# Attention in two halves: key scores two a step in steps 0 to 7, the next unit's query scores two a step in steps 7 to 14

## The chip, the cores and the metric

The kernel runs on one core of a Trainium2 chip. The time is that of the whole program on the device, in microseconds (us); the figure for a kernel is the median of several runs. The profiled execution is a run of its own with its own time. The engines are PE (TensorE, matmuls), DVE (VectorE), ACT (ScalarE), POOL (GpSimd) and SP (SyncE, which issues all DMAs here). Each works through its own instructions in order and waits on semaphores for the others.

## What is computed

One decoder layer on a batch of 8 sequences of 512 rows and 512 columns: self-attention with 16 heads of 32 columns, a retention layer, a coupling network; after each a residual sum and a layer norm. The change is in the attention alone:

```python
kv = (_ln(x, kvn_w, kvn_b) @ kv_w + kv_b).reshape(b, c, 2, HEAD, HD).transpose(2, 0, 3, 1, 4)
k, v = kv[0], kv[1]
q = (_ln(x, qn_w, qn_b) @ q_w + q_b).reshape(b, c, HEAD, HD).transpose(0, 2, 1, 3)
q, k = _rotary(q, x, rh_w, rh_b), _rotary(k, x, rh_w, rh_b)
qn, kn = _ln(q, ln_w, ln_b), _ln(k, ln_w, ln_b)
scores = jnp.einsum('bhqd,bhkd->bhqk', qn, kn) / np.sqrt(HD)
attn = jax.nn.softmax(scores, axis=-1)
a = jnp.einsum('bhqk,bhkd->bhqd', attn, v).transpose(0, 2, 1, 3).reshape(b, c, dims)
return a @ out_w + out_b
```

## The kernel before

The attention phase is 32 units U = 4b + g: batch b of 8, and g one of four groups of four heads. A unit has 16 steps, and tables at the top of the file (lines 31 to 42) say at which step each piece of work stands; every engine runs its own `unit` function over the same steps, so the tables set the order of instructions on each engine. All semaphore waits follow from that order.

Three units are in work at once. In unit U:

- For U itself PE does 16 *key scores* (line 741, bank `exp`), ACT an exponential for each (line 632), and after every four of them PE *weighs* (line 752): eight matmuls for the output and eight for the sums, both of a quarter of the array's width. DVE *normalises* in four chunks (lines 475 and 477), ACT and DVE split the result into a high and a low part (lines 639 and 486). `weigh` of the next unit's first quarter waits for that low part (line 748).
- For U + 1 PE does 16 *query scores* (line 726, banks `max0` and `max1`), DVE takes a row maximum of each (line 467). Query score i waits for maximum i - 2 (two banks). When all 16 are done PE transposes the maxima (line 732), ACT copies them into `stack` (`save_max`, line 623), and only then can the key scores of U + 1 begin (line 738).
- For U + 3 PE projects: 16 items of three matmuls (lines 703 to 705), four items for each of four row tiles t; DVE adds the bias (`save_qkv`, lines 431 and 433); tile t waits for the save of tile t - 2. POOL rotates.
- For U + 2 DVE takes means and variances of the heads (lines 439 and 449), POOL subtracts and scales (lines 305 to 320), PE turns the heads (line 714), ACT and DVE split them (`turn_high`, line 619; `turn_low`, line 458). After the second `turn_low` SP issues 24 DMAs that lay the parts of unit U + 2 out in `stack` (`regroup`, line 227). Query scores of a head wait for its six DMAs.

In the unit with g = 0 of batch b PE also multiplies the attention of batch b - 1 with the output weights (`project_out`, lines 760 to 762, four tiles of 12 matmuls), and transposes the normalised rows of batch b + 1 (line 696). In the unit with g = 1 SP, behind its 24 DMAs, loads residual rows (line 238) and then the rows `z` of batch b + 2 (line 241). In the unit with g = 2 DVE takes the statistics of these rows (`x_stats`, lines 382 and 383), whose first instruction waits for that load (line 381); this is done for b = 0 to 5. In the unit with g = 3 follow `x_final` and `x_shift`.

The loop over steps on DVE has this order within one step:

```python
row_max of U + 1; normalise (if its step is below 8); attn_low (line 486); head_mean; head_var;
save_qkv; turn_low; x_stats; x_final; x_shift; add_out; z_low; normalise (if its step is 8 or more)
```

and on PE: query scores, projection items, key scores, `weigh`, transposed maxima, turned heads, transposed rows, output products.

Of the kernel before, what the change touches and what calls it, by code (L numbers as in the profile page):

```python
# [19 lines left out]
B, S, D = 8, 512, 512  # L20
T = S // P
K = D // P
H, HD = 16, 32
G = 4
HG = H // G
# [2 lines left out]
DVE_STEPS, POOL_STEPS = 55, 40  # L28


QS_DONE = tuple(T * HG * min(i + 1, 14) // 14 for i in range(16))
KS_DONE = tuple(T * HG * min(i, 12) // 12 for i in range(16))
PROJECT_DONE = (3, 5, 6, 8, 10, 11, 13, 15, 16, 16, 16, 16, 16, 16, 16, 16)
WEIGH_AT = (5, 8, 11, 14)
TURN_AT, SAVE_AFTER = (9, 11), (2, 4, 7, 9)
OUT_AT, ADD_AFTER, OUT_BANK = (10, 12, 15, 15), (11, 13, 15, 15), (1, 1, 0, 1)
Z_AT, Z_HIGH_AT, Z_LOW_AFTER = (13, 13, 14, 14), (13, 13, 15, 15), (13, 14, 15, 15)
MAX_AT, SAVE_MAX_AT = 14, 14
X_NORM_AT, STATS_AFTER, FINAL_AFTER, SHIFT_AFTER = (5, 6, 7, 8), (6, 8, 10, 12), 6, 12
MEAN_AFTER, VAR_AFTER, SQUARE_AT = (0, 1), (3, 4), (1, 2)  # L40
TURN_HIGH_AT, TURN_LOW_AFTER = (10, 12), (11, 13)
NORM_AFTER, ATTN_HIGH_AT, ATTN_LOW_AFTER = (15, 15, 0, 1), 2, 3
SIDES = (1, 0)

ROW = 3 * HD
# [46 lines left out]
def attention_phase(nc, x, x1, w):  # L92
# [6 lines left out]
    with ctx:  # L99
# [264 lines left out]
        def _(dve):  # L364
# [105 lines left out]
            def normalise(W, c):  # L470

                at = slice(c * P, (c + 1) * P)
                if c == 0:
                    dve.wait_ge(pv_done, T * W + T)
                nc.vector.reciprocal(inverse[:, at], bank_sum[:, at]).then_inc(dve_step, 1)  # L475
                dve.wait_ge(dve_step, steps.next())
                last = nc.vector.tensor_tensor(bank_o[:, at], bank_o[:, at], inverse[:, at], ALU.mult)
                if c < T - 1:
                    last.then_inc(dve_step, 1)
                    dve.wait_ge(dve_step, steps.next())  # L480
                else:
                    last.then_inc(attn_done, 1)
# [12 lines left out]
            def unit(b, g, left, more):  # L495
                U = G * b + g
                for i in range(T * HG):
                    if left >= 1:
                        for m in within(QS_DONE, i):
                            row_max(U + 1, m)  # L500
# [83 lines left out]
            for s in range(2):  # L584
                turn_low(1, s, bank_t[s])
            run(dve, unit, steps, DVE_STEPS)
            for c in range(2, T):
                normalise(G * B - 1, c)
            attn_low(G * B - 1, G - 1)
            for t in range(T):  # L590
                add_out(B - 1, t)
# [2 lines left out]
        def _(act):  # L594
# [46 lines left out]
            def unit(b, g, left, more):  # L641
                U = G * b + g
                for i in range(T * HG):
                    for m in within(KS_DONE, i):
                        exps(U, m)
                    if i == ATTN_HIGH_AT and counts(U):
                        attn_hi(U - 1, (g - 1) % G)
                    for s in range(2):
                        if left >= 2 and i == SQUARE_AT[s]:
                            square(U + 2, s)  # L650
                        if left >= 2 and i == TURN_HIGH_AT[s]:
                            turn_high(U + 2, s, bank_t[0 if g == 0 else s])
                    for t in range(T):
                        if g == 0 and left == 4 and i == X_NORM_AT[t]:
                            x_norm(b + 1, t)
                        if g == 0 and left == 4 and i == Z_HIGH_AT[t]:
                            z_high(b + 1, t)
                    if i == SAVE_MAX_AT and left >= 1:
                        save_max(U + 1, (g + 1) % 2)

            act.wait_ge(load, 16 * len(loads))
            for t in range(T):
# [26 lines left out]
        def _(pe):  # L689
# [131 lines left out]
            def unit(b, g, left, more):  # L821
                U = G * b + g
                for i in range(T * HG):
# [6 lines left out]
                    for m in within(KS_DONE, i):  # L830
                        key_scores(U, g % 2, m)
                    if i in WEIGH_AT:
                        weigh(U, g, WEIGH_AT.index(i))
# [1105 lines left out]
```

## Time and profile before

| what | value |
|---|---|
| median of 3 runs | 2420.73 us (2419.41 to 2424.11) |
| profiled execution, its own time | 2423.02 us |
| its span | 2421.0 us |
| mean granted TensorE clock | 0.901 |
| PE busy | 1945.1 us (80%) |
| DVE busy | 1546.8 us (64%) |
| ACT busy | 908.2 us (38%) |
| POOL busy | 951.5 us (39%) |

The attention phase fills about the first 1300 us of the span. A row of a timeline gives the start, the duration, the engine, the line, the operation with the names of the tiles, how many instructions were merged (x), and in brackets for how long the engine had been idle and what released it. Matmuls overlap: the start of one to the start of the next is what it really takes, not the duration shown. PEclk is the granted clock as a share of 2.4 GHz; 0.5 is 1.2 GHz.

### The profile page before, as it was taken

How to read it: one execution, taken by the hardware profiler on the slowest of the kernel's cores; microseconds unless marked ns; L12 is line 12 of the kernel's file. 1: busy time of each engine (PE TensorE's matmuls, PEld its weight loads, DVE VectorE, ACT ScalarE, POOL GpSimd, SP SyncE). 2: the span in 40 equal slices, each digit the busy share in tenths (PEclk: the TensorE clock that was granted, in tenths of full speed). 3: DMA queues.
4: the chain of work that ended last, by engine and by line, in shares of the span. 5: the costliest groups of instructions: out<-in, count | busy, mean ns of one | idle time of the engine just before them, and what ended most of it. 6: DMA issues, size and time to landing. Idle time of an engine off the chain costs nothing. (4 is left out here: it accounts for less than half of the span.)

```text
span 2421.0 us, 30214 instructions
## 1 busy us (share of the span) xinstructions
PE 1945.1 (80%) x9560; PEld 1426.2 (59%) x9560; DVE 1546.8 (64%) x2943; ACT 908.2 (38%) x1532; POOL 951.5 (39%) x849
## 2 busy tenths in 40 slices
PE   4587887878888798788975799999948887788772
PEld 4455565555656465565633688888837665666651
DVE  4567667576675666767562666667654776767765
ACT  2143433334333343334341322222214555555653
POOL 1666756467564674746620222222201212221221
PEclk9688998989989898999987899999979999989985
DMA  3123132131311212222122211211031121022111
GB/s 128 26 53 87 37 94 48 48 85 36 95 47 50 77 36 74 69 57 70 38 77 101 78 53 60 79 69 53 18 107 37 52 70 49 22 69 70 53 35 52
DMA packets 90746, 148.67 MB, mean 61 GB/s; under 512 B 16560, under 2 KB 19632, under 8 KB 90672
## 3 DMA queue, kind: packets, MB, share of 16 engines
q1 hardware_dynamic: 90672, 147.76, 20.5%
q8 instruction: 37, 0.61, 0.1%
q14 instruction: 37, 0.30, 0.0%
HBM read 63.82 MB, written 33.55 MB: 40 GB/s over the span
## 5 line engine op out<-in xcount | busy, mean ns | idle before, releaser
L467 DVE TENSOR_REDUCE a_neg_max<-a_max 128x1 f32<-128x512 f32 x512 | 344.5, 687 | 267.3 <-PE a_max L726 258.8
L632 ACT ACTIVATE a_probs<-a_exp 128x512 f32<-128x512 f32 x512 | 290.7, 595 | 571.1 <-PE a_exp L741 568.5
L726 PE MATMUL a_max<-a_stack 96*128 96x512 f32 x512 | 235.9, 476 | 150.7 <-DMA a_stack<-a_nT_lo 100.6
L726 PEld LDWEIGHTS a_max<-a_stack 96*128 96x128 f32 x512 | 103.2, 206 | 245.4 <-DMA a_stack<-a_nT_lo 106.8
L1497 POOL TENSOR_TENSOR f_mixed<-f_tw,f_beta 128x512 f32<-128x512 f32 x64 | 96.1, 1522 | 352.2 <-DVE f_beta L1596 177.0
L311 POOL TENSOR_TENSOR a_rstd<-a_rstd,a_minus_half 128x16 f32<-128x16 f32 x64 | 186.5, 2914 | 85.0 <-DVE a_rstd L452 85.0
L703 PE MATMUL a_t<-a_w_hi,a_zT_hi 128*128 128x384 f32 x512 | 196.5, 384 | 13.4 <-DVE a_v L433 11.5
L741 PE MATMUL a_exp<-a_stack 100*128 100x512 f32 x512 | 193.5, 419 | 6.5 <-ACT a_probs L632 4.5
L704 PE MATMUL a_t<-a_w_lo,a_zT_hi 128*128 128x384 f32 x512 | 194.8, 380 | 0.0
L705 PE MATMUL a_t<-a_w_hi,a_zT_lo 128*128 128x384 f32 x512 | 193.0, 377 | 0.0
L305 POOL TENSOR_TENSOR a_n<-a_n,a_mean 128x512 f32<-128x512 f32 x64 | 67.2, 1050 | 309.8 <-DVE a_mean L441 309.6
L1767 PE MATMUL f_l<-f_h_hi,f_w_hi 128*128 128x512 f32 x240 | 111.3, 464 | 73.1 <-DVE f_h_lo L1510 72.4
L1047 POOL TENSOR_TENSOR r_part<-r_part 128x512 f32<-128x512 f32 x32 | 45.8, 1432 | 315.1 <-DVE r_part L1094 315.1
L752 PE MATMUL a_o<-a_probs,a_v 128*32 128x512 f32 x1024 | 140.7, 622 | 3.3 <-ACT a_probs L632 0.9
L475 DVE RECIPROCAL a_inverse<-a_sum 128x128 f32<-128x128 f32 x128 | 121.8, 951 | 30.4 <-PE a_sum L752 29.2
L752 PE MATMUL a_sum<-a_probs,a_ones 128*32 128x512 f32 x1024 | 137.2, 608 | 0.0
L703 PEld LDWEIGHTS a_t<-a_w_hi,a_zT_hi 128*128 128x128 f32 x512 | 114.1, 223 | 23.8 <-DVE a_v L433 13.0
L1510 DVE TENSOR_TENSOR f_h_lo<-f_full,f_h_hi 128x512 fp32r<-128x512 f32 x104 | 70.4, 689 | 81.2 <-ACT f_h_hi L1675 80.5
L704 PEld LDWEIGHTS a_t<-a_w_lo,a_zT_hi 128*128 128x128 f32 x512 | 114.0, 223 | 13.5
L1169 ACT ACTIVATE r_kq_hi<-r_part 128x512 fp32r<-128x512 f32 x64 | 36.8, 624 | 218.7 <-POOL r_part L1048 218.7
L741 PEld LDWEIGHTS a_exp<-a_stack 100*128 100x128 f32 x512 | 101.9, 201 | 26.3 <-ACT a_probs L632 13.6
L705 PEld LDWEIGHTS a_t<-a_w_hi,a_zT_lo 128*128 128x128 f32 x512 | 113.5, 222 | 0.0
(240 smaller groups left out, 4865.7 us busy)
## 6 DMA issues: line engine op xcount, KB each, us to landing
a_stack<-a_nT_hi SPq DMA_DIRECT2D x512, 64.0 KB, 2.0
a_stack<-a_nT_lo SPq DMA_DIRECT2D x256, 64.0 KB, 2.0
a_z<-x SPq DMA_DIRECT2D x8, 1024.0 KB, 7.4
a_y<-x SPq DMA_DIRECT2D x8, 1024.0 KB, 5.5
x<-a_y SPq DMA_DIRECT2D x8, 1024.0 KB, 4.4
r_xn<-x SPq DMA_DIRECT2D x8, 1024.0 KB, 5.6
r_cn<-ctx SPq DMA_DIRECT2D x8, 1024.0 KB, 7.7
x<-r_xn SPq DMA_DIRECT2D x8, 1024.0 KB, 4.3
```

The lines of the kernel that those rows point to most:

```text
L311: nc.gpsimd.tensor_tensor(rstd[:, c], rstd[:, c], minus_half[:, :], ALU.pow).then_inc(pool_step, 1)
L467: nc.vector.tensor_reduce(neg_max[:, t, ROW + h:ROW + h + 1], bank_max[i % 2][:, :], AX_X, ALU.max, negate=True).then_inc(max_done, 1)
L475: nc.vector.reciprocal(inverse[:, at], bank_sum[:, at]).then_inc(dve_step, 1)
L632: nc.scalar.activation(probs[:, kt % 2, h, :], bank_exp[i % 2][:, :], ACT.Exp, scale=float(1.0 / np.sqrt(np.float32(HD)))).then_inc(exp_do ...
L703: mm(bank, zT_hi[:, k, at], w_hi[:, k, g, :], start=k == 0, stop=False)
L704: mm(bank, zT_hi[:, k, at], w_lo[:, k, g, :], start=False, stop=False)
L705: last = mm(bank, zT_lo[:, k, at], w_hi[:, k, g, :], start=False, stop=k == K - 1)
L726: mm(bank_max[i % 2][:, :], stack[0:ROW, par, h, t * P:(t + 1) * P], stack[0:ROW, par, HG + h, :], start=True, stop=True).then_inc(score_d ...
L741: mm(bank_exp[i % 2][:, :], stack[0:ROW + HG, par, HG + h, kt * P:(kt + 1) * P], stack[0:ROW + HG, par, h, :], start=True, stop=True).then ...
L752: last = mm(bank[at, :], ones[:, :] if sums else v[:, g, kt, at], probs[:, kt % 2, h, :], start=kt == 0, stop=kt == T - 1, tile_position=( ...
L1497: nc.gpsimd.tensor_tensor(mixed[:, j % 2, :], tw[:, par, j, :], beta[:, :], ALU.mult).then_inc(product_done, 1)
L1767: mm(bank, a_hi, b_hi, start=first, stop=False)
```

## The change

The tables give every piece another step. Key scores stood about three in four steps in steps 1 to 12 and query scores about eight in seven in steps 0 to 13, so that the two alternated. Now all 16 key scores stand two a step in steps 0 to 7 and all 16 query scores two a step in steps 7 to 14. `weigh` moves from steps 5, 8, 11, 14 to 3, 5, 7, 9; the maxima are transposed in step 15; the first three chunks of `normalise` come in steps 12, 13 and 15 of the unit itself and the last in step 0 of the next; `x_stats` moves from steps 6, 8, 10, 12 to 0, 1, 2, 3 of the unit with g = 2; `x_norm`, `x_final`, the turned heads and the output products move by some steps. No instruction is added or left out.

```diff
-QS_DONE = tuple(T * HG * min(i + 1, 14) // 14 for i in range(16))
-KS_DONE = tuple(T * HG * min(i, 12) // 12 for i in range(16))
-PROJECT_DONE = (3, 5, 6, 8, 10, 11, 13, 15, 16, 16, 16, 16, 16, 16, 16, 16)
-WEIGH_AT = (5, 8, 11, 14)
-TURN_AT, SAVE_AFTER = (9, 11), (2, 4, 7, 9)
-OUT_AT, ADD_AFTER, OUT_BANK = (10, 12, 15, 15), (11, 13, 15, 15), (1, 1, 0, 1)
+KS_DONE = tuple(2 * min(i + 1, 8) for i in range(16))
+QS_DONE = tuple(2 * max(min(i - 6, 8), 0) for i in range(16))
+PROJECT_DONE = (3, 6, 8, 8, 10, 10, 12, 12, 14, 15, 16, 16, 16, 16, 16, 16)
+WEIGH_AT = (3, 5, 7, 9)
+TURN_AT, SAVE_AFTER = (11, 12), (2, 4, 7, 11)
+OUT_AT, ADD_AFTER, OUT_BANK = (11, 12, 15, 15), (12, 13, 15, 15), (1, 1, 0, 1)
...
-MAX_AT, SAVE_MAX_AT = 14, 14
-X_NORM_AT, STATS_AFTER, FINAL_AFTER, SHIFT_AFTER = (5, 6, 7, 8), (6, 8, 10, 12), 6, 12
+MAX_AT, SAVE_MAX_AT = 15, 15
+X_NORM_AT, STATS_AFTER, FINAL_AFTER, SHIFT_AFTER = (10, 10, 11, 11), (0, 1, 2, 3), 3, 12
...
-TURN_HIGH_AT, TURN_LOW_AFTER = (10, 12), (11, 13)
-NORM_AFTER, ATTN_HIGH_AT, ATTN_LOW_AFTER = (15, 15, 0, 1), 2, 3
+TURN_HIGH_AT, TURN_LOW_AFTER = (11, 12), (11, 13)
+NORM_AFTER, ATTN_HIGH_AT, ATTN_LOW_AFTER = (12, 13, 15, 0), 1, 1
...
-            for c in range(2, T):
-                normalise(G * B - 1, c)
+            normalise(G * B - 1, T - 1)
...
+                    if i == SAVE_MAX_AT and left >= 1:
+                        save_max(U + 1, (g + 1) % 2)
                     for t in range(T):
                         if g == 0 and left == 4 and i == X_NORM_AT[t]:
                             x_norm(b + 1, t)
                         if g == 0 and left == 4 and i == Z_HIGH_AT[t]:
                             z_high(b + 1, t)
-                    if i == SAVE_MAX_AT and left >= 1:
-                        save_max(U + 1, (g + 1) % 2)
```

DVE at the place where the first `x_stats` stands in the unit with g = 2, before (L467 is a row maximum, L382 and L383 the statistics of `z`):

```order
L467 TENSOR_REDUCE a_neg_max<-a_max 128x1
L463 REGISTER_ALU
L467 TENSOR_REDUCE a_neg_max<-a_max 128x1
L463 REGISTER_ALU
L467 TENSOR_REDUCE a_neg_max<-a_max 128x1
L381 ISA
L382 BN_STATS a_stats<-a_z 128x6
L383 SCALAR_TENSOR_TENSOR a_inverse,a_per_step<-a_z,a_rh_w 128x512
L386 REGISTER_ALU
L463 REGISTER_ALU
L467 TENSOR_REDUCE a_neg_max<-a_max 128x1
```

The same place now (L475 and L477 are the last chunk of `normalise`, L439 and L441 the first `head_mean`, L486 is `attn_low`):

```order
L475 RECIPROCAL a_inverse<-a_sum 128x128
L476 REGISTER_ALU
L477 TENSOR_TENSOR a_o<-a_o,a_inverse 128x128
L438 REGISTER_ALU
L439 TENSOR_REDUCE a_mean<-a_n 128x16
L440 REGISTER_ALU
L441 TENSOR_SCALAR a_mean<-a_mean 128x16
L381 ISA
L382 BN_STATS a_stats<-a_z 128x6
L383 SCALAR_TENSOR_TENSOR a_inverse,a_per_step<-a_z,a_rh_w 128x512
L386 REGISTER_ALU
L486 TENSOR_TENSOR a_attnT_lo<-a_o,a_attnT_hi 128x512
```

The statistics stood behind the seventh or eighth row maximum of the unit; they now stand ahead of all of them, and ahead of `attn_low`.

PE near the end of a unit with g = 1, before (L726 is a query score, L741 a key score, L752 `weigh`, L714 turned heads, L732 the transposed maxima):

```order
L714 MATMUL a_t<-a_ident,a_n 128x128 x4
L725 REGISTER_ALU
L726 MATMUL a_max<-a_stack 128x512
L741 MATMUL a_exp<-a_stack 128x512 x2
L725 REGISTER_ALU
L726 MATMUL a_max<-a_stack 128x512
L725 REGISTER_ALU
L726 MATMUL a_max<-a_stack 128x512
L746 REGISTER_ALU
L752 MATMUL a_o<-a_probs,a_v 32x512 x4
L752 MATMUL a_sum<-a_probs,a_ones 32x512 x4
L732 MATMUL a_max<-a_ident,a_neg_max 100x128 x4
```

PE in the middle of a unit now (lines of this engine's part are lower by one: L725 is a query score, L740 a key score, L751 `weigh`, L702 to L704 a projection item):

```order
L740 MATMUL a_exp<-a_stack 128x512 x2
L720 REGISTER_ALU
L725 MATMUL a_max<-a_stack 128x512 x2
L740 MATMUL a_exp<-a_stack 128x512 x2
L751 MATMUL a_o<-a_probs,a_v 32x512 x4
L751 MATMUL a_sum<-a_probs,a_ones 32x512 x4
L724 REGISTER_ALU
L725 MATMUL a_max<-a_stack 128x512
L724 REGISTER_ALU
L725 MATMUL a_max<-a_stack 128x512
L770 REGISTER_ALU
L702 MATMUL a_t<-a_w_hi,a_zT_hi 128x384
```

The two kinds of scores no longer alternate; the first two query scores come just ahead of the last two key scores and the third `weigh`, and all others behind.

## Rows read from the trace of the kernel before

**Rows 1.** Windows of five units: length, PE, PEld, DVE, ACT, POOL busy, PEclk, DMA.

```profile
572.32:615.60 43.28, 39.02 (x222) 27.79 (x221) 23.43 (x44) 18.23 (x30) 20.22 (x19) 1.00 0.22 51
615.60:653.40 37.80, 30.65 (x157) 20.77 (x157) 26.66 (x52) 13.39 (x22) 22.23 (x21) 0.86 0.18 53
653.40:692.01 38.61, 30.69 (x157) 19.27 (x157) 26.99 (x57) 13.33 (x22) 24.99 (x22) 0.82 0.33 95
692.01:724.67 32.66, 28.60 (x157) 19.52 (x157) 24.34 (x56) 13.29 (x22) 24.57 (x23) 0.90 0.22 52
1111.46:1142.92 31.46, 27.33 (x157) 18.34 (x157) 22.27 (x45) 13.29 (x22) 23.37 (x22) 0.95 0.33 84
```

**Rows 2.** Groups by line: busy, mean ns | idle before, releasers.

```profile
L467 DVE TENSOR_REDUCE a_neg_max<-a_max 128x1 f32<-128x512 f32 x512 | 344.5, 687 | 267.3 <-PE a_max L726 258.8 <-DVE a_o L477 3.8 <-DVE a_inverse L383 1.1
L726 PE MATMUL a_max<-a_stack 96*128 96x512 f32 x512 | 235.9, 476 | 150.7 <-DMA a_stack<-a_nT_lo 100.6 <-DVE a_neg_max L467 48.5
```

**Rows 3.** PE's timeline across the end of a unit with g = 2.

```profile
681.43 0.64 PE L732 MATMUL a_max<-a_ident,a_neg_max 128*100 128x128 f32 x4
687.13 0.80 PE L726 MATMUL a_max<-a_stack 96*128 96x512 f32 x1 [5.05 <-DMA a_stack<-a_nT_lo]
692.01 0.39 PE L741 MATMUL a_exp<-a_stack 100*128 100x512 f32 x1
```

**Rows 4.** DVE's timeline: second turn_low of g = 1, first x_stats of g = 2.

```profile
642.76 0.68 DVE L458 TENSOR_TENSOR a_nT_lo<-a_t,a_nT_hi 128x512 fp32r<-128x512 f32 x1
...
666.99 0.69 DVE L382 BATCH_NORM_STATS2 a_stats<-a_z 128x6 f32<-128x512 f32 x1 [4.33 <-DMA a_z<-x]
...
668.40 0.69 DVE L467 TENSOR_REDUCE a_neg_max<-a_max 128x1 f32<-128x512 f32 x1
```

**Rows 5.** SP's timeline: first and last issue of regroup in g = 1, load of z.

```profile
643.47 0.53 SPq L227 DMA_DIRECT2D a_stack<-a_nT_hi  x1
...
657.98 0.59 SPq L227 DMA_DIRECT2D a_stack<-a_nT_lo  x1
...
659.52 0.38 SPq L241 DMA_DIRECT2D a_z<-x  x1
```

**Rows 6.** PE's timeline: weigh and items at full clock, weigh at half.

```profile
658.98 1.06 PE L752 MATMUL a_o<-a_probs,a_v 128*32 128x512 f32 x8
...
660.84 0.73 PE L726 MATMUL a_max<-a_stack 96*128 96x512 f32 x2
661.41 0.35 PE L703 MATMUL a_t<-a_w_hi,a_zT_hi 128*128 128x384 f32 x1
661.94 0.34 PE L703 MATMUL a_t<-a_w_hi,a_zT_hi 128*128 128x384 f32 x1
...
673.44 1.94 PE L752 MATMUL a_o<-a_probs,a_v 128*32 128x512 f32 x8
```

**Rows 7.** ACT's timeline: save_max, one exponential, three back to back.

```profile
682.11 1.87 ACT L623 ACTIVATE a_stack<-a_max 4x2048 fp32r<-4x2048 f32 x1 [2.29 <-PE a_max L732]
692.44 0.60 ACT L632 ACTIVATE a_probs<-a_exp 128x512 f32<-128x512 f32 x1 [8.46 <-PE a_exp L741]
695.54 1.78 ACT L632 ACTIVATE a_probs<-a_exp 128x512 f32<-128x512 f32 x3
```

**Rows 8.** Groups by line in the unit from 692.01 to 724.67.

```profile
L475 DVE RECIPROCAL a_inverse<-a_sum 128x128 f32<-128x128 f32 x5 | 4.8, 951 | 0.8 <-PE a_sum L752 0.8
L431 DVE TENSOR_TENSOR a_qk<-a_t,a_qkv_bias 128x256 f32<-128x256 f32 x4 | 1.7, 417 | 0.0
L477 DVE TENSOR_TENSOR a_o<-a_o,a_inverse 128x128 f32<-128x128 f32 x5 | 1.5, 300 | 0.2
```

**Rows 9.** PE's timeline at the end of a unit with g = 0.

```profile
602.89 0.64 PE L732 MATMUL a_max<-a_ident,a_neg_max 128*100 128x128 f32 x4
...
606.84 0.50 PE L760 MATMUL a_t<-a_wo_hi,a_attnT_hi 128*128 128x512 f32 x1 [2.43 <-DVE a_zT_lo L422]
...
612.28 0.39 PE L762 MATMUL a_t<-a_wo_hi,a_attnT_lo 128*128 128x512 f32 x1
```

## The prediction

> **What bounds the kernel now.** I read first the windows by unit [rows 1], since every engine's order repeats unit by unit. A batch of four units takes 152.3 us. No engine fills its unit: in the one from 692.01 PE shows 28.6 of 32.7 us, DVE 24.3, POOL 24.6, ACT 13.3. So the order and its waits set the pace, not one engine. The units differ: g = 0 carries output products and transposes (43.3), g = 1 and 2 take 37.8 and 38.6, g = 3 32.7, and a unit of batch 6, where no `z` is loaded, 31.5. Then the groups by line [rows 2]: PE's largest wait in attention is for the DMAs that fill `stack`, 100.6 us ahead of query scores, and DVE waits 258.8 us for query scores. The timelines [rows 3, 4, 5] show where: a unit begins with a query score that waits 5.05 us for its DMAs, and the first `x_stats` waits 4.33 us for `z`.
>
> **What the change takes away.** Query scores now begin at step 7. SP starts `regroup` right after the second `turn_low` and is through with 24 issues in 15.1 us (643.47 to 658.57) [rows 5]; below the first query score comes some 19 us after that `turn_low`, and each head's DMAs are ahead of it. I cost the `stack` wait at nothing from here on: up to 100.6 us gone, over 31 units 3.2 each.
>
> **The regular unit, step by step.** Time 0 is the end of its predecessor's sixteenth row maximum. Prices at full clock: a score 0.23; an item of three matmuls 0.53 (661.41 to 661.94) and a `weigh` 1.86 (658.98 to 660.84) [rows 6]; an exponential 0.59 when they queue (1.78 for three), its result usable about 1.0 after its score's start (692.01, 692.44, 0.60) [rows 3, 7]; a row maximum 0.61 to 0.69 [rows 2]; a chunk of `normalise` 1.3 (0.95 and 0.30 with a wait between) and a `save_qkv` about 0.6 [rows 8]; a `turn_low` 0.68 [rows 4].
>
> First the boundary: transposed maxima, then `save_max` 0.68 after their start and 1.87 long [rows 3, 7]. That puts the first key score at 2.75; three items hide most of it. Steps 0 to 3: eight key scores wait for exponentials two before them, while ACT also does `attn_hi` and two squares, the second of which waits for POOL behind `attn_low` and the second mean on DVE. Key 7 goes at 8.4, `weigh` 0 at 8.6 to 10.5. Two items, keys 8 and 9 (12.0), key 10 behind exponential 8 (12.6), key 11, `weigh` 1 to 15.3, two items, keys 12 and 13 to 16.8. Query score 0 goes at 16.9. Keys 14 and 15 wait for exponentials 12 and 13; `weigh` 2 ends at 20.0. DVE has had its two maxima and a save by 18.9 and idles to 20.4: query 2 stands behind `weigh` 2. The same again at `weigh` 3 (22.5 to 24.4): maximum 6 starts at 24.8. From there DVE is the chain: ten maxima (6.5), the last save (0.6), two `turn_low` (1.3), two chunks of `normalise` in steps 12 and 13 (2.6), less what two banks allow PE to run ahead, and a short wait at the turned heads: the sixteenth maximum ends at 35.4. So a regular unit takes 35.5 us, against 32.7 and 31.5 for g = 3 and for batch 6, and 37.8 for g = 1. What is late in place of `stack` is DVE: its 10 us of maxima no longer run beside the key scores, and it has little to do in steps 0 to 6. POOL's 24.6 us [rows 1] fit inside 35.5; I cost its reordering at nothing. If its rotation (behind the fourth save, now step 11, before 9) sets the means of the next unit, up to 2 us a unit more; since the first half there waits for ACT anyway, I take 0.
>
> **g = 0.** In the second half the two output tiles cost PE 2.8 each (24 matmuls in 5.7 us, 606.84 to 612.5 [rows 9]), and each stands ahead of query scores that DVE waits for; with additions and `z_low` on DVE the sixteenth maximum ends near 43.0. The transposed maxima wait for a bank until 44.3; from there to the end of the last two output tiles it took 9.6 us (602.89 to 612.5) [rows 9], an order that is unchanged; three items, and the next key score at 55.3: a length of 52.5, against 43.3.
>
> **g = 2: the rows of z.** This is the largest term. `x_stats` now stands in step 0, ahead of `attn_low`, and `weigh` 0 waits for `attn_low`. `z` cannot come earlier: it is issued behind the 24 DMAs of `regroup`, 16.1 us after the end of `turn_low` in g = 1 (643.44 to 659.52), and DVE goes on with it at 666.99, 23.6 after that end [rows 4, 5]. In the new order that `turn_low` ends 2.5 us before time 0, so `z` is there at 21.0. `x_stats` takes 1.4 (666.99 to 668.40), `attn_low` 0.7: `weigh` 0 goes at 23.1 and not at 8.6, 14.5 later, and behind it are PE's items, all query scores and so everything. PE stands still for it; after the shorter wait of 5.05 us in [rows 3] its matmuls ran 0.80 long, and at half clock (1.2 GHz) half a `weigh` is 1.94 long where it is 1.06 at full clock (2.4 GHz) [rows 6]; I add 2. The unit takes 52, against 38.6. The remaining three `x_stats` and the delayed means lie on DVE in the first half, where it has room.
>
> [...]
>
> **The sum.** A full batch: 52.5 + 35.5 + 52 + 35.5 = 175.5 against 152.3, +23.2. Batches 1 to 5: +116. Batch 6 has no `z`: +9.2 - 2.3 + 4 + 4 = +15. Batch 0 has no output products, and its first key score no longer stands behind the first fill of `stack`: about +12. Batch 7 has no items and shrinks to few differences: +3. Together +146 at the prices of full clock. The granted clock in units that are less dense is lower: 0.82 with 30.7 busy of 38.6, 0.95 with 27.3 of 31.5 [rows 1]. The new unit has the same matmuls in 35.5. Bounds: nothing more, or, with a second half wholly at half clock, +4 (two `weigh` at +1.7, the rest partly hidden by DVE). I take +1, near the rows of today, +31 over 31 units. The phases behind attention are untouched. So +177 on the profiled execution's own 2423.0 (span 2421.0): 2600; the median is 2.3 lower, hence 2598.
>
> **The rivals.**
> 1. *Only the late z costs.* Regular units and g = 0 stay as long as now, because the freed `stack` waits pay for DVE's new idleness in full. For it: 3.2 us a unit are gone, and my regular unit differs from today's by only -2 to +4. Against: the two waits behind `weigh` and the serial boundary follow from the order. Then 6 times 13.4 (52 against 38.6), +80: 2500.
> 2. *The clock falls.* DVE paces the second half, PE runs in short bursts and is granted 1.2 GHz through most of it: +4 a unit in place of +1, some +93 more: 2690. [...] The rows agree in direction (0.82 to 0.95 above), but a clock of 1.00 with 39.0 busy of 43.3 and 0.90 with 28.6 of 32.7 leave most units at the full level.
> 3. *Faster.* The query scores no longer wait for `stack`, and the halves overlap better than I have it: DVE's work of one unit's end runs beside the next one's key scores, and a regular unit comes down to what PE has at full clock (32 scores 7.4, 16 items 8.4, four `weigh` 7.4, turns and maxima 1.3) plus the boundary and two waits, 28. A batch is then 28 x 4 + 16 + 17 = 145, -7; over the phase about -40: 2380. It decides from a regular unit below 29.8, (152.3 - 33) / 4. For it: PE has 24.5 us of work. Against: it would need DVE to do the 15 us between query 0 and maximum 15 without a wait, and ACT to be no bound in steps 0 to 3. The late `z` remains even so.
>
> **How the numbers follow.** A difference of 0.2%, about 5 us, is what a measurement can tell from none. Forecast 0.52, with its own range 2545 to 2655; only the late z 0.25; the clock 0.13; faster 0.08; the remaining 0.02 is a coincidence of gains and losses within 0.2%. Slower is 0.90, same 0.02, faster 0.08. The range leaves out the faster case and the far part of the clock case: 2480 to 2695.
>
> **What would show it.** In the profile after: one wait of DVE's line 382 for `z` of 15 to 18 us in each of six batches, where it is 4.33 now; PE's wait of the same place some 14 us, ahead of `weigh`, with half clock behind it. No wait of query scores for `stack` beyond a few us. Row maxima that wait for query scores twice in a unit, at the third and fourth `weigh`. Units from key score to key score near 52, 35, 52, 35. I am wrong if `z` lands within a few us of DVE's arrival, if regular units are under 32, or if they are over 38 at a clock above 0.85.

## The result: 12% slower, and 116 us slower than forecast

| | before | changed |
|---|---|---|
| median, run side by side | 2422.42 us (2419.41 to 2427.52, 4 runs) | 2713.65 us (2711.63 to 2715.52, 4 runs) |
| ratio, 95% interval | 1 | 1.120 (1.1177 to 1.1222) |
| profiled execution, its span | 2423.02, 2421.0 | 2715.52, 2713.5 |
| mean granted TensorE clock | 0.901 | 0.867 |

The direction was as forecast. The size was not: +291 us where the text had +177, and the time lies above the range's upper end of 2695.

The busy times and the instruction queue, from the profile page of the changed kernel:

```profile
PE 2071.6 (76%) x9560; PEld 1437.7 (53%) x9560; DVE 1554.1 (57%) x2943; ACT 905.9 (33%) x1532; POOL 944.6 (35%) x849
...
q14 instruction: 62, 0.51, 0.1%
```

PE shows 126 us more of busy time for the same 9560 matmuls. At half clock they run longer: eight matmuls of a `weigh` 1.94 us in place of 1.06 (below). The row of q14, one of the two queues of the kind `instruction`, was not read ahead of the prediction. It counts 62 packets; the page of before has 37.

Windows of the four units of batch 3, of a unit of batch 6, and of the phase from the first key score of all to the last unit's (columns as in [rows 1]):

```profile
690.08:746.66 56.58, 45.69 (x222) 30.34 (x221) 25.00 (x46) 18.25 (x30) 20.98 (x20) 0.88 0.20 46
746.66:792.04 45.38, 32.98 (x157) 19.04 (x157) 24.80 (x49) 13.28 (x22) 21.57 (x21) 0.86 0.12 36
792.04:845.57 53.53, 34.31 (x158) 20.09 (x157) 28.46 (x56) 13.17 (x22) 23.14 (x22) 0.76 0.25 69
845.57:884.55 38.98, 31.87 (x158) 19.33 (x157) 24.26 (x55) 13.16 (x22) 24.89 (x25) 0.89 0.17 41
...
1368.23:1406.47 38.24, 31.69 (x157) 19.12 (x157) 23.25 (x44) 13.16 (x22) 22.81 (x22) 0.90 0.27 69
...
121.98:1564.15 1442.17, 1089.38 (x5172) 655.64 (x5171) 769.23 (x1507) 442.02 (x733) 675.89 (x632) 0.85 0.19 49
```

The same stretch of the kernel before:

```profile
131.07:1269.18 1138.11, 961.81 (x5165) 642.43 (x5164) 756.16 (x1497) 444.22 (x733) 677.35 (x625) 0.91 0.24 62
```

The phase is 304 us longer and starts 9 us earlier; what lies behind it is 2.5 us shorter. All four kinds of units grew, and the fourth kind, the last row but one, is what a unit costs in which nothing is special: 38.2 us, against 31.5 in [rows 1]. From the mean clock c of a stretch of length L one gets the time at the lower of the two levels (PEclk 0.50) as 2(1 - c)L: about 2 x 0.09 x 1138 = 205 us before and 2 x 0.15 x 1442 = 433 us now. That there are two levels is what short windows show: of 3793 windows of 0.3 us in this stretch of the kernel before, 3095 have a PEclk of 1.00 and 627 one of 0.50; of 4806 in that of the changed kernel, 3277 and 1441; the rest lie between the two.

The groups by line, which answer to [rows 2]:

```profile
L467 DVE TENSOR_REDUCE a_neg_max<-a_max 128x1 f32<-128x512 f32 x512 | 329.4, 685 | 346.4 <-PE a_max L725 340.4
...
L725 PE MATMUL a_max<-a_stack 96*128 96x512 f32 x512 | 222.4, 485 | 69.3 <-DVE a_neg_max L467 59.7
...
L751 PE MATMUL a_o<-a_probs,a_v 128*32 128x512 f32 x1024 | 148.5, 654 | 79.1 <-DVE a_attnT_lo L486 79.1
```

The 100.6 us that query scores waited for `stack` are gone, as forecast. In their place DVE waits 340.4 us for query scores (258.8 before), and PE 79.1 us for `attn_low`, in six waits.

**The late `z`.** DVE's timeline: the second `turn_low` of g = 1, the first `x_stats` of g = 2, and `attn_low` behind it:

```profile
784.93 0.68 DVE L458 TENSOR_TENSOR a_nT_lo<-a_t,a_nT_hi 128x512 fp32r<-128x512 f32 x1
...
809.15 0.69 DVE L382 BATCH_NORM_STATS2 a_stats<-a_z 128x6 f32<-128x512 f32 x1 [17.62 <-DMA a_z<-x]
...
810.48 0.69 DVE L486 TENSOR_TENSOR a_attnT_lo<-a_o,a_attnT_hi 128x512 fp32r<-128x512 f32 x1
```

SP's timeline between them, and PE's at the same place:

```profile
785.64 0.54 SPq L227 DMA_DIRECT2D a_stack<-a_nT_hi  x1
...
801.69 0.38 SPq L241 DMA_DIRECT2D a_z<-x  x1
```

```profile
811.31 1.94 PE L751 MATMUL a_o<-a_probs,a_v 128*32 128x512 f32 x8 [12.90 <-DVE a_attnT_lo L486]
```

From the end of `turn_low` to the first `x_stats` are 23.6 us, the number of [rows 4, 5]. PE stands for 12.90 us where 14.5 were booked, and `weigh` behind it runs at half clock: half of it is 1.94 long where it is 1.06 at full clock [rows 6].

**The regular unit.** PE's timeline in batch 6, g = 2; the prediction's time 0 is 1364.32 here, where the sixteenth maximum ends:

```profile
1364.46 1.09 PE L731 MATMUL a_max<-a_ident,a_neg_max 128*100 128x128 f32 x4 [2.32 <-DVE a_neg_max L467]
...
1366.31 0.52 PE L702 MATMUL a_t<-a_w_hi,a_zT_hi 128*128 128x384 f32 x1
...
1367.27 0.52 PE L702 MATMUL a_t<-a_w_hi,a_zT_hi 128*128 128x384 f32 x1
...
1368.23 1.05 PE L740 MATMUL a_exp<-a_stack 100*128 100x512 f32 x2
...
1374.84 1.06 PE L751 MATMUL a_o<-a_probs,a_v 128*32 128x512 f32 x8
...
1383.39 0.63 PE L725 MATMUL a_max<-a_stack 96*128 96x512 f32 x2
```

and DVE's, later in the unit:

```profile
1387.37 1.29 DVE L467 TENSOR_REDUCE a_neg_max<-a_max 128x1 f32<-128x512 f32 x2 [1.73 <-PE a_max L725]
...
1392.05 2.63 DVE L467 TENSOR_REDUCE a_neg_max<-a_max 128x1 f32<-128x512 f32 x4 [1.88 <-PE a_max L725]
...
1402.57 0.95 DVE L475 RECIPROCAL a_inverse<-a_sum 128x128 f32<-128x128 f32 x1
```

The items at the boundary follow each other in 0.96 us, at half clock, where 0.53 was booked [rows 6]. The first key score comes at 3.9 (booked 2.75), `weigh` 0 at 10.5 (8.6), query 0 at 19.1 (16.9), maximum 6 at 27.7 (24.8), and the sixteenth ends at 38.25 (35.4). The two waits behind `weigh` 2 and 3 are there, 1.73 and 1.88. Two thirds of the loss of 2.85 us have arisen by `weigh` 0: 1.2 up to the first key score, and 0.8 more between that and `weigh` 0.

The lower level does not begin with the wait of 2.32 us ahead of the transposed maxima, which lasts from 1362.14 to 1364.46. It begins earlier, among the last query scores, where PE waits for row maxima. PE's windows and timeline there:

```profile
1349.01:1359.25 10.24, 9.29 (x48) 5.08 (x46) 7.95 (x14) 1.19 (x2) 2.12 (x3) 1.00 0.00 0
1359.25:1369.49 10.24, 6.49 (x20) 5.39 (x20) 8.20 (x15) 2.41 (x3) 7.54 (x11) 0.50 0.29 66
```

```profile
1358.32 1.01 PE L725 MATMUL a_max<-a_stack 96*128 96x512 f32 x2 [0.63 <-DVE a_neg_max L467]
1360.75 1.39 PE L725 MATMUL a_max<-a_stack 96*128 96x512 f32 x2 [1.42 <-DVE a_neg_max L467]
```

Two scores took 1.01 us there, and the next two 1.39.

**A hole that nobody releases.** DVE's timeline at the start of the unit with g = 1:

```profile
746.95 0.30 DVE L477 TENSOR_TENSOR a_o<-a_o,a_inverse 128x128 f32<-128x128 f32 x1
753.03 0.96 DVE L475 RECIPROCAL a_inverse<-a_sum 128x128 f32<-128x128 f32 x1 [5.78 <-issue]
```

Between two chunks of `normalise` DVE stands still for 5.78 us and waits for nothing that the profile shows (the releaser is "issue"). PE's key scores behind it then wait 6.58 us for an exponential. The loop over batches runs six times, and each pass begins with the unit with g = 1; the hole stands behind each of the five jumps back (5.78 to 5.83 us), and nowhere else in DVE's program of this phase. 62 - 37 = 25 more packets of instructions are five a jump. The trace also records the branches: at each of these jumps DVE's next instruction starts 5.40 to 5.44 us behind the branch, and 0.26 to 0.30 behind it in the kernel before. The unit takes 45.4 us in batches 1 to 5, and 37.9 in batch 6, behind the loop.

### The profile page after: what moved, and what is told of

Read it like the earlier page. It is cut to its first block and busy times, and to the rows that moved or that the text cites. A ratio compares the mean times of both kernels' runs of the same rounds, so it can differ in the third digit from the quotient of the medians.

```text
span 2713.5 us, 30240 instructions
## 1 busy us (share of the span) xinstructions
PE 2071.6 (76%) x9560; PEld 1437.7 (53%) x9560; DVE 1554.1 (57%) x2943; ACT 905.9 (33%) x1532; POOL 944.6 (35%) x849
## 5 line engine op out<-in xcount | busy, mean ns | idle before, releaser
L467 DVE TENSOR_REDUCE a_neg_max<-a_max 128x1 f32<-128x512 f32 x512 | 329.4, 685 | 346.4 <-PE a_max L725 340.4
L631 ACT ACTIVATE a_probs<-a_exp 128x512 f32<-128x512 f32 x512 | 277.9, 596 | 296.1 <-PE a_exp L740 289.4
L725 PE MATMUL a_max<-a_stack 96*128 96x512 f32 x512 | 222.4, 485 | 69.3 <-DVE a_neg_max L467 59.7
L740 PE MATMUL a_exp<-a_stack 100*128 100x512 f32 x512 | 209.7, 467 | 80.9 <-ACT a_probs L631 76.6
L702 PE MATMUL a_t<-a_w_hi,a_zT_hi 128*128 128x384 f32 x512 | 202.0, 395 | 16.2 <-DVE a_v L433 11.7
L751 PE MATMUL a_o<-a_probs,a_v 128*32 128x512 f32 x1024 | 148.5, 654 | 79.1 <-DVE a_attnT_lo L486 79.1
L725 PEld LDWEIGHTS a_max<-a_stack 96*128 96x128 f32 x512 | 95.3, 197 | 194.8 <-DVE a_neg_max L467 125.6
L740 PEld LDWEIGHTS a_exp<-a_stack 100*128 100x128 f32 x512 | 103.1, 206 | 163.0 <-ACT a_probs L631 150.4
L704 PE MATMUL a_t<-a_w_hi,a_zT_lo 128*128 128x384 f32 x512 | 188.4, 368 | 0.0
L702 PEld LDWEIGHTS a_t<-a_w_hi,a_zT_hi 128*128 128x128 f32 x512 | 111.3, 217 | 81.6 <-issue 52.2
L475 DVE RECIPROCAL a_inverse<-a_sum 128x128 f32<-128x128 f32 x128 | 121.5, 949 | 45.3 <-issue 29.0
L751 PE MATMUL a_sum<-a_probs,a_ones 128*32 128x512 f32 x1024 | 145.3, 641 | 0.0
L622 ACT ACTIVATE a_stack<-a_max 4x2048 fp32r<-4x2048 f32 x32 | 59.8, 1870 | 251.3 <-PE a_max L731 251.3
L287 POOL TENSOR_TENSOR a_turn<-a_qk,a_cos 128x256 f32<-128x256 f32 x64 | 47.5, 742 | 273.9 <-DVE a_v L433 273.9
L618 ACT ACTIVATE a_nT_hi<-a_t 128x512 fp32r<-128x512 f32 x64 | 38.2, 597 | 313.1 <-PE a_t L713 313.0
```

Of the source, the lines that this page charges most:

```text
L467: nc.vector.tensor_reduce(neg_max[:, t, ROW + h:ROW + h + 1], bank_max[i % 2][:, :], AX_X, ALU.max, negate=True).then_inc(max_done, 1)
L631: nc.scalar.activation(probs[:, kt % 2, h, :], bank_exp[i % 2][:, :], ACT.Exp, scale=float(1.0 / np.sqrt(np.float32(HD)))).then_inc(exp_do ...
L702: mm(bank, zT_hi[:, k, at], w_hi[:, k, g, :], start=k == 0, stop=False)
L704: last = mm(bank, zT_lo[:, k, at], w_hi[:, k, g, :], start=False, stop=k == K - 1)
L725: mm(bank_max[i % 2][:, :], stack[0:ROW, par, h, t * P:(t + 1) * P], stack[0:ROW, par, HG + h, :], start=True, stop=True).then_inc(score_d ...
L740: mm(bank_exp[i % 2][:, :], stack[0:ROW + HG, par, HG + h, kt * P:(kt + 1) * P], stack[0:ROW + HG, par, h, :], start=True, stop=True).then ...
```

## The experiments

After the result there were four places to which 291 us could belong: the late `z`; the hole behind the jump back; DVE's and PE's other work in the second half; and what remains when all these are taken away, the order of two halves and the clock that it leaves. Numbers 1, 4, 5, 10 and 11 ask for the first (theory A: it costs its full time wherever it stands), 2, 3 and 9 for the second (theory C: it belongs to the loop's place among the instructions, not to its work), 6, 7 and 12 for the third (theory F: DVE's chunks), 8 and 11 for the last. The times of before beside each are those of runs on the same chip, 2422 to 2428 us. In the expectations `after_late` is number 1, `halves_norm` number 6 and `early_q2` number 8.

**1. The statistics one unit later.** `z` is then there long before it is wanted.

```diff
-                    if g == 2 and more and i in STATS_AFTER:
+                    if g == 3 and more and i in STATS_AFTER:
```

> The changed kernel with x_stats in steps 0 to 3 of the unit with g = 3 instead of g = 2, so that DVE never stands for the load of z ahead of attn_low. Theory A (the late z is the largest single cost of the change): the wait of line 382 goes, a unit with g = 2 falls from 53.5 to the 38.2 us that it takes in batch 6 where no z is loaded, six times 15.3, so 2714 - 92 = 2622 us; four statistics (5.6 us of DVE) fit in the first half of g = 3, where DVE waits anyway. Theory B (DVE's work is what is short, not z): g = 3 grows by the 5.6 us, six times, and the gain is 58 us: 2656.

Measured: 2611.61 us, ratio 1.0773 (1.0749 to 1.0797), 102 less than the changed kernel. The unit with g = 2 shrinks from 53.5 to 38.4 us. The late `z` costs about 15 us six times, and no other wait takes its place.

**2. DVE's loop four places earlier.** The unit written out ahead of the loop now has three chunks of `normalise` instead of two (steps 12, 13 and 15 against 15 and 15), so that the loop begins later in DVE's program. DVE does the same 2943 instructions of work in both kernels, but with waits and register instructions counted, the trace has 576 of DVE's records ahead of the first branch back where it had 569, and 377 in a pass of the loop where it had 374. So the loop begins four instructions later, and not two, and its end stands seven later. Four copies instead of eight ahead of the loop do the same work with four instructions less:

```diff
-            for half in range(2):
-                for h in range(HG):
-                    last = nc.vector.tensor_copy(stack[ROW:ROW + HG, half, HG + h, :],
-                                                 ident[ROW:ROW + HG, ROW + h:ROW + h + 1].broadcast_to((HG, S)))
+            for h in range(HG):
+                last = nc.vector.tensor_copy(stack[ROW:ROW + HG, :, HG + h, :],
+                                             ident[ROW:ROW + HG, ROW + h:ROW + h + 1].unsqueeze(1).broadcast_to((HG, 2, S)))
```

> The changed kernel with four instead of eight copies on DVE ahead of the attention loop (two stack halves in one copy), so that the loop begins four instructions earlier; nothing in the loop is touched. [...] Theory D (the hole is a wait that the profile doesn't name): unchanged, 2714.

Measured: 2677.26 us, ratio 1.1046 (1.1022 to 1.1071), 36 less; five units that fall from 45.4 to the 37.9 of batch 6 would give 37.5. From its page, and the window of batch 4, g = 1:

```profile
q14 instruction: 37, 0.30, 0.0%
```

```profile
1107.77:1145.97 38.20, 31.55 (x157) 18.89 (x157) 24.88 (x49) 13.28 (x22) 21.54 (x21) 0.88 0.13 42
```

The 25 packets and the hole are gone, the unit falls from 45.4 to 38.2. The loop's work is unchanged, so the hole belongs to where the loop lies.

**3. The kernel before with two more instructions ahead of the loop.**

```diff
+            for i in range(2):
+                nc.vector.memset(pad[:, i:i + 1], 0.0)
```

> The kernel before with two one-column memsets on DVE ahead of the attention loop; nothing in the loop is touched. Theory C: 25 instruction packets more, a hole of about 6 us on DVE at each of five jumps back. There the next row maximum is what PE waits for, so up to 6 us each: 2422 + 30 = 2452 us. Theory D: unchanged, 2422.

Measured: 2425.81 us, ratio 1.0009 (0.9995 to 1.0023), 38 packets. No stop behind the jump back (0.24 to 0.30 us, the table under number 9) and no cost: two places alone don't do it in this kernel. The two were too few to reproduce the change, which moves the branch back by seven; number 9 goes further.

**4. The kernel before with the statistics in steps 0 to 3.**

```diff
-X_NORM_AT, STATS_AFTER, FINAL_AFTER, SHIFT_AFTER = (5, 6, 7, 8), (6, 8, 10, 12), 6, 12
+X_NORM_AT, STATS_AFTER, FINAL_AFTER, SHIFT_AFTER = (5, 6, 7, 8), (0, 1, 2, 3), 6, 12
```

> The kernel before with STATS_AFTER at steps 0 to 3 instead of 6, 8, 10, 12, and nothing else of the change. Theory A: z lands some 24 us after turn_low in this order too, DVE stands from about 6 us after it, PE stands at the third query score and at weigh 0; a unit with g = 2 grows by 13 to 18 us, six times: 2500 to 2530 us. Theory E (the alternating order absorbs the wait, since key scores and items run on): under 2450.

Measured: 2509.22 us, ratio 1.0355 (1.0328 to 1.0382), +85, near 14 us a load. Its table of waits:

```profile
DVE a_stats L382 <- DMA a_z<-x: 90.1, 6, 15.4
```

The units with g = 2 take 52 to 54 us where they took 37.5 to 40.5. So the early statistics cost nearly the same alone, in the old order.

**5. The load of `z` ahead of the 24 DMAs of `regroup`.**

```diff
+                if g == 1 and more:
+                    sp.wait_ge(zT_done, T * (b + 2))
+                    sp.dma_start(z[:, :, :], rows(x, b + 2)).then_inc(x_in, 16)
...
-                    if more:
-                        sp.wait_ge(zT_done, T * (b + 2))
-                        sp.dma_start(z[:, :, :], rows(x, b + 2)).then_inc(x_in, 16)
```

> The changed kernel with SP's load of z issued ahead of the 24 DMAs of regroup in the unit with g = 1 instead of behind them; all tables as in the change. Theory A (z is late because it is queued behind regroup, which waits for the second turn_low): z lands some 20 us before DVE wants it, no wait of line 382, units with g = 2 at 38, 2714 - 6 x 15.3 = 2622 us. Theory B (statistics ahead of attn_low cost by themselves, 4 x 1.4 us on DVE): g = 2 stays at 43 or more, 2650 us.

Measured: 2612.73 us, ratio 1.0767 (1.0736 to 1.0799), 101 less, the same as number 1 in another way. The unit with g = 2 takes 37.9. What makes `z` late is SP's queue, not the load.

**6. Numbers 1 and 2 together, and all of `normalise` off the query half.** 1 and 2 together are not run; their sum from the medians is 2713.65 - 102.0 - 36.4 = 2575.

```diff
-NORM_AFTER, ATTN_HIGH_AT, ATTN_LOW_AFTER = (12, 13, 15, 0), 1, 1
+NORM_AFTER, ATTN_HIGH_AT, ATTN_LOW_AFTER = (15, 15, 0, 1), 1, 1
```

> The changed kernel with x_stats in g = 3, the four copies ahead of the loop (the two edits tried before, worth 102 and 37 us: together 2575 us), and NORM_AFTER back at steps 15, 15, 0, 1, so that no chunk of normalise stands among the row maxima. Theory F (in the second half DVE is the chain, and what stands between its maxima adds in full): 2 x 1.3 us less a unit, 31 units, 2575 - 80 = 2495 us. Theory G (the chunks only move into the boundary, where attn_low and the means wait for them): 2575 us.

Measured: 2549.70 us, ratio 1.0505 (1.0477 to 1.0533), some 25 less than 2575, where 80 were expected. The unit with g = 2 fell from 38.3 to 35.1 as computed; g = 1 rose from 38.2 to 39.3, and g = 3, with the statistics in it, took 37.8 to 39.8 (38.4 in number 1). ACT's and PE's timelines in g = 1 show the price:

```profile
1011.04 0.60 ACT L638 ACTIVATE a_attnT_hi<-a_o 128x512 fp32r<-128x512 f32 x1 [2.47 <-DVE a_o L476]
```

```profile
1012.70 0.98 PE L740 MATMUL a_exp<-a_stack 100*128 100x512 f32 x2 [3.50 <-ACT a_probs L631]
```

`attn_hi` waits for the last chunk, and the exponentials stand behind `attn_hi` on ACT. The theory that DVE's chunks in the second half are what lengthens the units holds in one unit of four.

**7. And `weigh` of quarters 2 and 3 behind the query scores that DVE waits for.**

```diff
-WEIGH_AT = (3, 5, 7, 9)
+WEIGH_AT = (3, 5, 11, 13)
```

> As halves_norm, and WEIGH_AT (3, 5, 11, 13) instead of (3, 5, 7, 9). Theory F': each weigh among the first maxima leaves DVE idle for 1.7 to 1.9 us, because two banks hold less than its 1.86 us; at steps 11 and 13 DVE has save_qkv and turn_low beside it, the holes go: 2495 - 31 x 3.5 = 2387 us. Theory H (a hole stands wherever a weigh stands among query scores): 2495 us.

Measured: 2489.71 us, ratio 1.026 (1.0233 to 1.0287), 60 less than number 6: between the two expectations of -108 and none. DVE's timeline in the unit with g = 2 of batch 4:

```profile
1017.88 1.29 DVE L466 TENSOR_REDUCE a_neg_max<-a_max 128x1 f32<-128x512 f32 x2 [5.94 <-PE a_max L725]
1019.61 5.35 DVE L466 TENSOR_REDUCE a_neg_max<-a_max 128x1 f32<-128x512 f32 x8
```

Eight maxima stand back to back, without the two waits; the unit takes 33.4 us at a clock of 1.00. The mean over the phase rises to 0.94, from 0.90 in number 6. So the 60 us are those of the two waits and of the clock together, and no run parts them. Still the two halves cost 62 us more than the old order.

**8. The scores alternate as before, but query scores start at step 2 and end at step 14.** An edit of the kernel before: the maxima are transposed in step 15, with `save_max` ahead of `z_high`, and nothing else is moved.

```diff
-QS_DONE = tuple(T * HG * min(i + 1, 14) // 14 for i in range(16))
+QS_DONE = tuple(T * HG * min(max(i - 1, 0), 13) // 13 for i in range(16))
-MAX_AT, SAVE_MAX_AT = 14, 14
+MAX_AT, SAVE_MAX_AT = 15, 15
```

> The alternating order of the kernel before, with the query scores in steps 2 to 14 instead of 0 to 13 and the maxima transposed in step 15. Theory I (what the halves were right about is that query scores should begin later than their stack DMAs): the 100.6 us of waits for stack go, most of it gained, 2422 - 80 = 2342 us. Theory J (the maxima are then the chain, ending two steps later, and the boundary is exposed): 2422 us or more.

Measured: 2390.55 us, ratio 0.9852 (0.9825 to 0.988). Faster, but by 37 us (1.5%) and not by the 80 expected. The `stack` wait of PE is gone (7.4 us are left of 100.6); the wait for `z` grew:

```profile
DVE a_stats L382 <- DMA a_z<-x: 49.2, 6, 9.6
```

It was 24.3 us in six waits, 4.7 at most. A gain of the units before g = 2 had been spent on reaching the same transfer earlier: that unit takes 39.5 to 42.7 us, g = 1 and g = 3 about 32.4 and 28.4.

**9. Eight instructions ahead of the loop of the kernel before** (as number 3, with `range(8)`).

> The kernel before with eight one-column memsets on DVE ahead of the attention loop (two made no difference and fetched no more instructions). [...] Theory D' (it is not the position of the loop but something of its content in the changed kernel): 2422 us, no more packets.

Measured: 2442.54 us, ratio 1.007 (1.0053 to 1.0087). From its page, and DVE's timeline behind a jump back:

```profile
q14 instruction: 62, 0.51, 0.1%
```

```profile
632.49 0.69 DVE L470 TENSOR_REDUCE a_neg_max<-a_max 128x1 f32<-128x512 f32 x1 [5.26 <-issue]
```

The same 25 packets and the same kind of hole, 5.26 us long here and 4.45 to 5.38 over the five jumps, with nothing changed in the loop. It costs 16 us here and 36 in the changed kernel: in the old order the unit loses 3.8 us (41.6 against 37.8) behind a hole of 4.5 to 5.4, in the new one 7.2 behind 5.8. Put beside each other, the traces of all kernels fall into two groups by the number of DVE's records ahead of the first branch back:

| kernels | records ahead of the first branch back | packets of q14 | from branch to next instruction |
|---|---|---|---|
| before, numbers 2 to 4, 6 to 8, 10, 11 | 568 to 572 | 37 or 38 | 0.24 to 0.30 us |
| changed, numbers 1, 5, 9, 12 | 576 or 577 | 62 or 63 | 4.06 to 6.57 us |

Number 3 stands at 571, the changed kernel at 576, number 2 at 572 and number 9 at 577. So from 572 to 576 something is passed that costs the packets and the stop, in both orders. No run stands between these two; and whether the start of the loop or its end decides, the runs don't tell.

**10. `z` first in the kernel before** (the edit of number 5).

> The kernel before with that edit alone. Theory A: 24.3 us of waits of DVE go; units with g = 2 fall from 38 to at most the 31.5 us of batch 6, up to 6 x 6 = 36 us: 2390 us. Theory L (DVE's 4.3 us there is mostly covered): 2410 us or more.

Measured: 2391.51 us, ratio 0.986 (0.9843 to 0.9876). The unit with g = 2 falls from about 38.5 to 34.3.

**11. Numbers 8 and 10 together.**

> early_q2 (alternating order, query scores in steps 2 to 14) with the load of z issued ahead of regroup in g = 1. In early_q2 the six waits for z have grown to 49 us in all and the units with g = 2 take 42.7 or 40 where 28.8 without a load. Theory A: they fall to 29, so 2390 - 6 x 12.5 = 2315 us. Theory K (the loads would then take bandwidth from regroup, and the query scores wait for stack again): 2370 us or more.

Measured: 2331.94 us, ratio 0.9619 (0.9596 to 0.9642): the fastest of all, 95 us below the kernel before. Windows of batch 5:

```profile
811.21:858.61 47.40, 41.47 (x222) 28.60 (x221) 26.18 (x50) 18.35 (x30) 22.93 (x22) 0.96 0.27 65
858.61:890.73 32.12, 28.34 (x158) 18.03 (x157) 23.62 (x46) 13.47 (x22) 21.21 (x20) 0.95 0.21 67
890.73:921.15 30.42, 27.30 (x157) 16.77 (x157) 27.59 (x57) 13.46 (x22) 24.27 (x22) 1.00 0.34 88
921.15:950.00 28.85, 27.01 (x157) 16.75 (x157) 23.61 (x55) 13.48 (x22) 23.50 (x23) 1.00 0.22 52
```

PE is busy 124 of 139 us and at its full level nearly throughout. Together the two edits bring 95, apart 37 and 35: once `stack` no longer holds the unit up, `z` first is worth more (59 us, 2390.55 to 2331.94). PE's timeline at the boundary between two units, to be held against that of the regular unit above:

```profile
887.64 0.64 PE L732 MATMUL a_max<-a_ident,a_neg_max 128*100 128x128 f32 x4
...
890.73 0.39 PE L741 MATMUL a_exp<-a_stack 100*128 100x512 f32 x1
```

PE comes to the transposed maxima straight from a `weigh`, at full clock, and the first key score follows in 3.09 us with no wait.

**12. Number 1 with fewer items at the boundary.** One item instead of three between the transposed maxima and the first key score, in case the items themselves hold that score up.

```diff
-PROJECT_DONE = (3, 6, 8, 8, 10, 10, 12, 12, 14, 15, 16, 16, 16, 16, 16, 16)
+PROJECT_DONE = (1, 4, 6, 8, 10, 10, 12, 12, 14, 15, 16, 16, 16, 16, 16, 16)
```

> after_late (2611.6 us) with one projection item instead of three in step 0, and the other two spread so that step 3 ends at the same count: PROJECT_DONE (1, 4, 6, 8, ...). Theory M (at the start of a unit TensorE stands at half clock, an item takes 0.96 us and three outlast save_max, so that the first key score goes at 3.9 us behind the last row maximum instead of 2.75): the first key score goes 1.0 to 1.2 us sooner and the unit is that much shorter, 30 units with items or less: 2611 - 30 = 2580 us. Theory N (ACT and the weigh behind it bound steps 0 to 3, the boundary is not on the chain): 2611 us.

Measured: 2634.59 us, ratio 1.0864 (1.0832 to 1.0896), 23 more than number 1. PE's timeline in one unit:

```profile
1281.51 1.09 PE L731 MATMUL a_max<-a_ident,a_neg_max 128*100 128x128 f32 x4 [2.32 <-DVE a_neg_max L467]
...
1284.57 1.22 PE L740 MATMUL a_exp<-a_stack 100*128 100x512 f32 x2 [1.00 <-ACT a_stack L622]
...
1288.46 1.05 PE L740 MATMUL a_exp<-a_stack 100*128 100x512 f32 x2
...
1290.70 0.63 PE L740 MATMUL a_exp<-a_stack 100*128 100x512 f32 x2
```

The first key score came 3.06 us behind the transposed maxima instead of 3.77, as meant, but PE then idled 1.00 us, and half clock lasted until about 1290, through the two items and more that had been moved behind that score. In this unit the lower level ended 8.5 us behind the start of the transposed maxima, and 5.0 behind it in number 1. Over the phase the clock fell from 0.88 to 0.85. Neither expectation was right: the items at the boundary cost time at half clock, and taking them away costs more.

## Why the prediction was wrong in size

Units, averaged over batches 1 to 5, with what was booked (the clock's +1 included):

| unit | before | booked | measured | in number 2 (`after_fit`) |
|---|---|---|---|---|
| g = 0 | 43.9 | 53.5 | 56.6 | 56.7 |
| g = 1 | 37.8 | 36.5 | 45.4 | 38.2 |
| g = 2 | 38.5 | 53.0 | 53.6 | 53.8 |
| g = 3 | 32.2 | 36.5 | 38.9 | 39.0 |

The gap between the forecast for the profiled execution, 2600, and its 2715.5 splits as follows.

- **Nothing in the sum for a jump back: 36 us** (5 x 7.2; 36.4 by the medians of number 2). This step failed entirely. The text said that no instruction is added, and counted only what stands in a unit. But the third chunk of `normalise` had moved across the start of the loop, the loop itself holds three more of the instructions that do no work (waits and register instructions), and with that the loop lies elsewhere. Shown by numbers 2 and 9, and by the two groups of traces under number 9.
- **The clock term was mis-sized: about 39 us in batches 1 to 5, 6 in batch 6.** Booked was +1 a unit. Measured over the booking were +3.1 for g = 0, +1.7 for g = 1 without the hole, +0.6 for g = 2 and +2.4 for g = 3. In the regular unit 1.2 of 2.85 us had arisen by the first key score, at the boundary, where nine matmuls took 0.32 each in place of 0.175; the text priced them at full clock. Another 0.8 came by `weigh` 0, in steps that the prediction has bound by ACT's exponentials; the level was still the lower one for the first 1.3 us of them. In g = 0 the stretch from the transposed maxima to the end of the output tiles took 11.7 us for the booked 9.6, with its first matmuls 0.43 apart, the last ones 0.23, and the first of them 0.4 us later behind the maxima than in [rows 9] (PE's timeline):

```profile
733.36 1.06 PE L731 MATMUL a_max<-a_ident,a_neg_max 128*100 128x128 f32 x4
737.73 0.79 PE L759 MATMUL a_t<-a_wo_hi,a_attnT_hi 128*128 128x512 f32 x1 [3.31 <-DVE a_zT_lo L422]
738.32 0.63 PE L760 MATMUL a_t<-a_wo_lo,a_attnT_hi 128*128 128x512 f32 x1
738.75 0.63 PE L761 MATMUL a_t<-a_wo_hi,a_attnT_lo 128*128 128x512 f32 x1
...
744.62 0.40 PE L760 MATMUL a_t<-a_wo_lo,a_attnT_hi 128*128 128x512 f32 x1
744.85 0.40 PE L761 MATMUL a_t<-a_wo_hi,a_attnT_lo 128*128 128x512 f32 x1
```

  Number 12 shows how tightly this hangs together: less work at the boundary, and the half level lasted longer. The rival of the clock had the right place and too high a price. It said that PE, run in short bursts in the second half, stands at half clock through most of it. In the changed kernel the level fell in the last part of that half, in batches 1 to 6 from 2.4 to 5.7 us ahead of the transposed maxima on, and stayed down until 3.7 to 8.1 us behind them; in the units with a late `z` it was down for 17.1 us more, around PE's wait. In number 7, where two `weigh` stand among these last query scores, the same boundary in batch 6, with the transposed maxima at 1193.22, stayed at the full level (PEclk 1.00). That sparse work of PE there is the cause is argued from this, not shown. The prediction's own sign of error came true: over 38 us for a regular unit (38.2) at a clock above 0.85 (0.90); as 38.2 is only just over, this sign is weak. That all of the missing 39 us is the clock is argued from these rows, not shown; no run holds the clock still.
- **Batches 0 and 7: 17 and 20 us.** They were booked by judgement at +16 and +6 with the clock, not step by step. In batch 0 the unit with g = 2 has a late `z` too, 53.5 against 37.5 us: the text named six batches, but +12 holds no room for the sixth. In batch 7 there are no items to put between the scores, and the three units with a successor grew by 14.1, 2.5 and 9.6 us (48.3, 37.0, 34.5 against 34.2, 34.5, 24.9). A unit without filler doesn't shrink to few differences: its halves stand one behind the other.

These sum to 36 + 39 + 6 + 17 + 20 = 118, less the 2.5 us behind the phase.

What held: the `stack` wait went (100.6 us), the two waits behind `weigh` 2 and 3 came (1.73 and 1.88 us), and number 7 shows that they and their place are real. The **late `z`** was the largest single term: 101 and 102 us by two independent edits, 17 for each of six loads, of which 15.2 lie in the unit with g = 2 itself (53.6 against 38.4 in number 1); booked were 16.5 (52 against 35.5). That the whole unit came out so near, 53.6 for 53, is in part luck: its regular part was 1.9 us longer than the 36.5 booked (38.4), and what `z` added was 1.3 us shorter. The load took 7.46 us from its issue at 801.69 to DVE's start at 809.15, as before the change (7.47) [rows 4, 5]. The first rival, that it alone costs, is refuted by the same runs: without it the kernel is still at 2612. Held, too, the reading that DVE, with little to do in steps 0 to 6 and all maxima behind, sets the second half's pace: numbers 6 and 7 took 85 us in all, by moving DVE's and PE's other work within that half or out of it; how much of it is the clock, as said, is not parted.

What the numbers above leave is the order itself. With `z` in time, the hole gone, and `normalise` and `weigh` moved, two halves take 2489.71 us. With `z` in time too, scores that alternate (four key scores in three steps, eight query scores in seven) take 2391.51, number 10, and 2331.94 when the query scores also start two steps later, number 11. So like for like the halves cost 98 to 158 us, more than the 62 against the kernel before. It is not the clock, which is 0.94 over the phase in number 7 and 0.93 in number 10. What it is instead is argued and not shown: the faster rival had the halves overlap better, while in the traces the row maxima no longer run beside the key scores, and overlap is what the change removes.

## What to carry to other kernels

A wait for a resource can be removed by starting its user a little later; number 8 needed two steps, and moving everything behind seven went with a lower clock and longer waits (0.85 against 0.91 over the phase, and DVE 340.4 us idle for query scores against 258.8). For each instruction that moves earlier, follow its operand back to the queue that issues the transfer: here the load stood behind 24 issues of 0.63 us, and putting it first was worth 35 us before and 59 us after the other gain. And if anything crosses the start of a hardware loop, look at the packets of the instruction queues in the profile before comparing anything else.

## What the runs showed of the hardware

- A loop's jump back can cost a stop of 4.1 to 6.6 us on one engine, between the branch and the next instruction, where it is 0.24 to 0.30 us otherwise. With it come 5 packets of about 8 KB on an instruction queue ((0.51 - 0.30) MB for 25). It depends on where the loop lies in the engine's program: 37 or 38 packets and no stop with 568 to 572 of DVE's records ahead of the first branch back, 62 or 63 packets with 576 or 577. The engine that stands still shows "issue" as its releaser.
- A stretch at half clock (PEclk 0.50) of 6.8 to 13.7 us lay around the transposed maxima of each unit of the changed kernel in batches 1 to 6. In the regular unit it began at 1359.25, behind a wait of 0.63 us and ahead of those of 1.42 and 2.32 us; an item's matmul took 0.32 us until 1369.4 and 0.175 from 1369.6 on. In number 11, where PE came to the same place without a wait, it stayed at full clock (PEclk 1.00 around 887.64). In the 10.24 us ahead of the fall in the regular unit PE was busy for 9.29; what makes the level fall, no run shows. Moving filler away from the boundary, number 12, made the lower level last longer (8.5 us behind the start of the transposed maxima, 5.0 in number 1) and the kernel 23 us slower.
